# Selective scan: C's rows split into bfloat16 parts in 128x64 tiles, and laid into the spreading table by transfers

## The chip, the cores and the metric

The kernel runs on one core of a Trainium2 chip. The metric is the device time of one execution in microseconds (us); a change is judged by the median of several executions. PE is the matrix engine (PEld its weight loads), DVE the vector engine, ACT the scalar engine, POOL the GpSimd engine, SP the engine that here only issues transfers. SPq and ACTq are the instruction queues of SP and ACT when they issue a DMA.

## The reference, cut to what matters

Four transformer-like layers with an attention-like and an expert block each, on x of shape (8, 512, 128). The change lies in the attention-like block of the third layer, a Mamba block (`L2_attn`), for a batch of 8 sequences of length 512 with 256 inner channels and 16 states:

```python
xdbl = jnp.einsum('bld,de->ble', xc, W_xproj)
dt_r = xdbl[..., :DT_RANK]
Bm = xdbl[..., DT_RANK:DT_RANK + D_STATE]
Cm = xdbl[..., DT_RANK + D_STATE:]
dt = jax.nn.softplus(jnp.einsum('blr,rd->bld', dt_r, W_dt) + b_dt)
A = -jnp.exp(A_log)

def step(h, inp):
    dt_t, B_t, C_t, u_t = inp
    dA = jnp.exp(dt_t[:, :, None] * A)
    h = h * dA + dt_t[:, :, None] * B_t[:, None, :] * u_t[:, :, None]
    y = jnp.einsum('bdn,bn->bd', h, C_t)
    return (h, y)
```

What is computed stays the same: C's values are needed on all 128 partitions, and a float32 value is carried through a bfloat16 matmul as the sum of three bfloat16 parts.

## The kernel before, in words

`build` runs seven layers one after the other, with a barrier between them. `selective_scan` (L2637) is the fifth. Channels lie on partitions in two halves (CH = 2), the sequence of 512 positions along the free axis. The work is a row of M = 128 steps m = 16 q + n: sequence q (0 to 7), state n (0 to 15). A step consists of

- a transfer issued by SP (L2716) that brings B's row n of sequence q from DRAM to all partitions, into one of NB = 4 buffers `bs`;
- on POOL, `dBu` = du * B (L2784), 128x1024, at most ND = 3 steps ahead of the recurrence;
- on ACT, `decay` (L2921), dA = exp(dt * A) in two halves, at most NA = 2 steps ahead;
- on DVE, `recur` (L3020), the scan h over the positions, and for 13 of 16 states `weigh` (L3029), hc = h * C. C's row comes from a bank of PSUM that PE fills by `spread` (L3124), one matmul of the 0/1 table `pick` with `bc`, the spreading table of bfloat16 parts. For the other three states (n = 0, 3, 6) POOL does the multiplication (L2731), with C's row brought by a transfer of SP (L2721) into `c_rows`;
- on PE, `add_up` (L3141), which sums hc into the bank of y.

Between these steps each engine does its part of the preparation of later sequences, at fixed values of n. B and C of sequence q+1 come so: PE's `project` (L3108) makes dt_r, B and C; ACT's `take_bc` (L2871, L2874) copies them from PSUM at n = 0 (at n = 2 for sequence 1) and issues the transfer that stores B and C in DRAM (`b_rows`, L2877). Then the split: `split_first` on ACT (L2882) rounds the 32x512 tile to bfloat16 straight into `bc`, `split_left` on POOL (L2736) takes the remainder, `split_mid` (L2886, ACT) rounds it, `split_last` (L2740, POOL) takes the second remainder, and `split_done` (L2890, L2891, ACT) writes the second and third part into `bc`.

Each engine works its instructions in the order in which they are written, and so does each queue: SP issues one transfer after the other, and where it waits for a semaphore, all transfers written behind wait too. SP waits for `dBu_ready` before it fills a `bs` buffer again (L2715), for the store of B and C at n = 0 (L2713), and for `hp_ready` before it fills `c_rows` again (L2720).

## Time and profile before

| | us |
|---|---|
| median of 3 runs | 2778.79 |
| lowest and highest run | 2772.78 and 2779.42 |
| the profiled execution, its own time | 2771.78 |
| its span in the profile | 2770.0 |
| selective scan, first scan of DVE to last | 900.4 to 1327.0 |
| DVE busy in 1003 to 1057 (one sequence) | 51.77 of 54 |

Times in the profile count from the start of the span. A row of a view names engine, line of the source, operation, output and inputs, and shapes; "xN" is the number of instructions merged in it. Idle time in brackets is what the engine stood still before the row, and behind "<-" stands what ended it.

### The profile page before, as it was taken

What the parts mean: (1) busy time and instruction counts of PE and PEld (TensorE: products, weight loads), DVE (VectorE), ACT (ScalarE), POOL (GpSimd) and SP (SyncE); (2) the same over time, 40 slices, a digit from 0 to 9 for tenths busy, and PEclk for the clock granted to TensorE, in tenths of its full rate; (3) what the DMA queues carried; (4) which work ended last, traced back from release to release, by engine and by line L of the source; (5) the groups of instructions that cost most, each with busy time, mean ns of one, the idle gap of its engine ahead of it and who ended that gap; (6) DMA issues with size and microseconds to landing.
All of it is one profiled execution on the core that took longest, in us unless ns stands there. A gap on an engine that the chain in (4) does not pass through costs nothing. (4 is left out here: it accounts for less than half of the span.)

```text
span 2770.0 us, 42642 instructions
## 1 busy us (share of the span) xinstructions
PE 2480.3 (90%) x13253; PEld 1589.3 (57%) x13280; DVE 1740.7 (63%) x4100; ACT 1433.8 (52%) x2908; POOL 1615.9 (58%) x1421
## 2 busy tenths in 40 slices
PE   7977787799578899997579899999999999999999
PEld 4756777687565344433379734444444445777776
DVE  4436444575424999999756599999999992211112
ACT  3431333334246877775334377777777774333333
POOL 4742555442364999999145376777767771997000
PEclk9988999899788999999889999999999999999999
DMA  9011333500012232322520068888888884000001
GB/s 295 25 35 49 109 107 108 165 1 24 26 40 73 93 98 91 96 97 88 175 80 25 14 142 196 192 191 191 191 195 187 194 193 100 9 16 9 8 8 31
DMA packets 148262, 274.82 MB, mean 99 GB/s; under 512 B 29003, under 2 KB 68694, under 8 KB 148038
## 3 DMA queue, kind: packets, MB, share of 16 engines
q1 hardware_dynamic: 135798, 251.75, 35.2%
q0 software_dynamic: 9088, 18.63, 2.4%
q8 instruction: 109, 1.79, 0.3%
q10 hardware_dynamic: 3152, 1.71, 0.3%
q14 instruction: 115, 0.94, 0.1%
HBM read 102.97 MB, written 24.58 MB: 46 GB/s over the span
## 5 line engine op out<-in xcount | busy, mean ns | idle before, releaser
L1784 POOL TENSOR_TENSOR l3a_p_all<-l3a_p_all,l3a_rden 128x1024 f32<-128x1024 f32 x256 | 483.7, 1893 | 202.2 <-DVE l3a_rden L1859 202.1
L1917 ACT ACTIVATE l3a_p_all<-l3a_p_all,l3a_low 128x512 f32<-128x512 f32 x512 | 364.3, 713 | 129.8 <-DVE l3a_low L1854 128.5
L1854 DVE CUSTOM_DVE_ANT_0 l3a_p_all<-bank,relative_bias 128x512 f32<-128x512 f32 x512 | 331.9, 686 | 53.9 <-PE bank L1983 30.5
L1867 DVE STREAM_TRANSPOSE l3a_blocks<-l3a_p_all 128x1024 f32<-128x1024 f32 x256 | 313.9, 1235 | 1.8 <-issue 1.8
L2784 POOL TENSOR_TENSOR l2a_dBu<-l2a_du,l2a_bs 128x1024 f32<-128x1024 f32 x128 | 298.5, 2352 | 17.4 <-DVE l2a_h L3020 16.2
L3020 DVE TENSOR_TENSOR_SCAN l2a_h<-bank,l2a_dBu 128x1024 f32<-128x1024 f32 x128 | 290.9, 2281 | 11.9 <-POOL l2a_dBu L2784 6.5
L1841 DVE SCALAR_TENSOR_TENSOR x<-bank,l3a_blocks,x 128x128 f32<-128x128 f32 x256 | 71.9, 344 | 336.5 <-PE bank L2058 336.3
L1932 ACT ACTIVATE relative_bias<-bank,l3a_b 128x512 f32<-128x512 f32 x224 | 153.3, 687 | 214.1 <-PE bank L2048 210.8
L1983 PE MATMUL bank<-l3a_kT,l3a_qT 64*128 64x512 f32 x1024 | 245.3, 607 | 3.1 <-DVE l3a_low L1854 2.6
L2009 PE MATMUL bank<-l3a_pT,l3a_v 128*64 128x512 f32 x1024 | 233.8, 598 | 0.1
L2048 PE MATMUL bank<-relative_xnT_all,relative_w_qk 128*128 128x512 f32 x512 | 231.0, 595 | 0.0
L2058 PEld LDWEIGHTS bank<-relative_w_qk,relative_bias 128*128 128x128 f32 x1792 | 208.1, 192 | 25.1 <-issue 25.1
L2058 PE MATMUL bank<-relative_w_qk,relative_bias 128*128 128x128 f32 x1792 | 208.5, 275 | 1.0 <-DVE x L1841 1.0
L3141 PE MATMUL bank<-l2a_hc,ident 128*128 128x512 f32 x416 | 202.9, 612 | 2.5 <-DVE l2a_hc L3029 1.9
L2921 ACT ACTIVATE bank<-l2a_dt,scan_a_neg 128x511 f32<-128x511 f32 x256 | 165.3, 681 | 70.6 <-DVE l2a_h L3020 67.1
L1983 PEld LDWEIGHTS bank<-l3a_kT,l3a_qT 64*128 64x128 f32 x1024 | 98.3, 187 | 148.9 <-issue 139.0
L2048 PEld LDWEIGHTS bank<-relative_xnT_all,relative_w_qk 128*128 128x128 f32 x512 | 93.2, 192 | 93.9 <-issue 93.9
L2009 PEld LDWEIGHTS bank<-l3a_pT,l3a_v 128*64 128x64 f32 x1024 | 67.8, 136 | 120.1 <-issue 111.9
L1207 POOL DMA_INDIRECT l0f_y_rows<-l0fe_y,l0f_target x71 | 75.7, 1066 | 95.5 <-DVE l0fe_y L1276 71.3
L1989 PE MATMUL bank<-relative_xnT_all,relative_w_qk 128*128 128x512 f32 x256 | 128.7, 626 | 2.9 <-issue 2.9
L3141 PEld LDWEIGHTS bank<-l2a_hc,ident 128*128 128x128 f32 x416 | 78.8, 193 | 87.7 <-issue 82.1
L3029 DVE TENSOR_TENSOR l2a_hc<-l2a_h,bank 128x1024 f32<-128x1024 f32 x104 | 124.7, 1199 | 3.7 <-PE bank L3124 3.0
(532 smaller groups left out, 4964.3 us busy)
## 6 DMA issues: line engine op xcount, KB each, us to landing
l3a_pT<-l3a_blocks SPq DMA_DIRECT2D x1024, 128.0 KB
l2a_bs<-l2a_b_rows SPq DMA_DIRECT2D x128, 256.0 KB, 3.1
l0fe_wv<-expert_weights SPq DMA_DIRECT2D x71, 256.0 KB
by_place<-by_distance SPq DMA_DIRECT2D x16, 512.0 KB, 12.6
relative_bias<-by_place SPq DMA_DIRECT2D x16, 448.0 KB, 11.3
...
```

The lines of the kernel that those rows point to most:

```text
L1784: p_ready.by(pool.tensor_tensor(a, a, bcast(rden[g % 2][:, t, :], n_after=S), ALU.mult))
L1854: bk.drain(dve.tensor_tensor_reduce(p_of(g, t)[:, h, :], ps(job)[:], bias[:, u * 2 + h, b0:b0 + S], 1.0, 3.0e38, ALU.add, ALU.min, low[:, ...
L1867: ins = dve.transpose(out, p_of(g, t).rearrange("p h (k b j) -> p (h k) b j", b=Q, j=32))
L1917: ins = act.activation(a, a, ACT.Exp, bias=low[:, t, h:h + 1], scale=-1.0, accum_out=den[:, t, h:h + 1])
L1983: bk.fill(pe.matmul(ps(job)[:], qT[half[h], t * P:(t + 1) * P], kT[half[h], :], start=True, stop=True), job)
L2009: ins = pe.matmul(ps(job)[half[h], :], v[g // GP % 2][:, kt, c:c + DK3], pT[g % 2][:, :, h * TPS + kt, :], start=(kt == 0), stop=(kt == TP ...
L2048: bk.fill(pe.matmul(ps(job)[:], w1[e % 2][:, j * P:(j + 1) * P], xnT_all[:, q * S:(q + 1) * S], start=True, stop=True), job)
L2058: ins = pe.matmul(ps(job)[:, t * D:(t + 1) * D], h[q][:, j, t * P:(t + 1) * P], w2[e % 2][:, j, :], start=(j == 0), stop=(j == J - 1))
L2784: pool.tensor_tensor(dBu[m % ND][:], du[q % 2][:], bcast(bs[m % NB][:], n_before=CH), ALU.mult).then_inc(dBu_ready, 1)
L2921: ins = act.activation(dA[m % NA][:, j, 1:], dt[q % 2][:, j, 1:], ACT.Exp, scale=a_neg[:, j, n:n + 1])
L3020: dve.tensor_tensor_scan(h[m % NH][:].rearrange("p c s -> p (c s)"), dA[m % NA].rearrange("p c s -> p (c s)"), dBu[m % ND][:].rearrange("p ...
L3141: ins = pe.matmul(y_bank[j][:], chip.ident[:], weighed[:, j, :], start=False, stop=(m % N == N - 1))
```

## The change

The tile `raw` (C and B, 32x512) is still copied out of PSUM and stored in DRAM. The split is no longer made on it. SP fetches C's 16 rows back from DRAM as a tile `c_flat` of 128 partitions x 64 elements (each row in 8 pieces); the two remainders on POOL and three roundings on ACT work on 128x64 tiles; and ACT then issues three transfers that lay the three parts into `bc`, 16 rows of 8 pieces of 64 bfloat16 values each. B's rows are no longer split (their rows of `bc` keep the zeros). The steps of the split are moved to later n. The core of the difference:

```diff
@@ -2659,7 +2659,9 @@
         turned = [sb(f"turned{u}", [P, TAPS - 1 + S]) for u in range(3)]
         xc, sz, work = two("xc", [P, CH, S]), sb("sz", [P, CH, S]), sb("work", [P, CH, S])
         dt, du = two("dt", [P, CH, S]), two("du", [P, CH, S])
-        raw, dtr, left, mid = sb("raw", [2 * N, S]), sb("dtr", [R, S]), sb("left", [2 * N, S]), sb("mid", [2 * N, S], BF16)
+        raw, dtr = sb("raw", [2 * N, S]), sb("dtr", [R, S])
+        CUT = N * S // P
+        c_flat, c_left, c_parts = sb("c_flat", [P, CUT]), sb("c_left", [P, CUT]), sb("c_parts", [P, 3, CUT], BF16)
         bc = two("bc", [P, S], BF16)
         bs = [sb(f"bs{k}", [P, S]) for k in range(NB)]
         dBu, h, hc = ([sb(f"{n}{k}", [P, CH, S]) for k in range(c)] for n, c in (("dBu", ND), ("h", NH), ("hc", NC)))
@@ -2706,11 +2709,18 @@
         with nc.Block(no_gpsimd_drain=True) as block:
             @block.sync
             def _(sp):
+                def load_flat(q):
+                    sp.wait_ge(b_stored, 16 * (q + 1))
+                    if q:
+                        sp.wait_ge(left_ready, q)
+                    sp.dma_start(c_flat[:], b_rows[q, N:2 * N, :].rearrange("n (c s) -> (n c) s", s=CUT)).then_inc(flat_loaded, 16)
+
                 answers.load(sp, (0,))
+                load_flat(0)
                 for m in range(M):
                     q, n = divmod(m, N)
-                    if n == 0:
-                        sp.wait_ge(b_stored, 16 * (q + 1))
+                    if n == 5 and q + 1 < B:
+                        load_flat(q + 1)
                     if m >= NB:
                         sp.wait_ge(dBu_ready, m - NB + 1)
                     sp.dma_start(bs[m % NB][:], b_rows[q, n, :].partition_broadcast(P)).then_inc(b_loaded[m % NB], 16)
@@ -2731,13 +2741,15 @@
                     pool.tensor_tensor(hp[k % 2][:], h[m % NH][:], bcast(c_rows[k % 2][:], n_before=CH), ALU.mult).then_inc(hp_ready, 1)
 
                 def split_left(q):
+                    pool.wait_ge(flat_loaded, 16 * (q + 1))
                     pool.wait_ge(hi_ready, q + 1)
-                    pool.wait_ge(raw_ready, q + 1)
-                    pool.tensor_tensor(left[:], raw[:], bc[q % 2][0:2 * N, :], ALU.subtract).then_inc(left_ready, 1)
+                    if q:
+                        pool.wait_ge(low_ready, q)
+                    pool.tensor_tensor(c_left[:], c_flat[:], c_parts[:, 0, :], ALU.subtract).then_inc(left_ready, 1)
 
                 def split_last(q):
                     pool.wait_ge(mid_ready, q + 1)
-                    pool.tensor_tensor(left[:], left[:], mid[:], ALU.subtract).then_inc(left2_ready, 1)
+                    pool.tensor_tensor(c_left[:], c_left[:], c_parts[:, 1, :], ALU.subtract).then_inc(left2_ready, 1)
 
                 def add_step(q, part):
@@ -2785,9 +2797,9 @@
                     if m == 2:
                         late_gains()
                     if q + 1 < B:
-                        if n == (5 if q else 7):
+                        if n == (9 if q else 10):
                             split_left(q + 1)
-                        if n == 10:
+                        if n == (12 if q else 13):
                             split_last(q + 1)
                         if n == 12:
                             add_step(q + 1, slice(0, CH))
@@ -2866,29 +2878,37 @@
                 def take_bc(q):
                     job = ("bc", q)
                     bk.wait_filled(act, job, 0)
-                    if q:
-                        act.wait_ge(left2_ready, q)
                     act.copy(dtr[:], ps(job)[2 * N:2 * N + R, :]).then_inc(dtr_ready, 1)
                     if q:
                         act.wait_ge(b_stored, 16 * q)
                     bk.drain(act.copy(raw[:], ps(job)[0:2 * N, :]), job)
                     bk.wait_read(act, job, 0)
                     act.sem_inc(raw_ready, 1)
+                    act.wait_ge(raw_ready, q + 1)
                     act.dma_start(b_rows[q], raw[:]).then_inc(b_stored, 16)
 
                 def split_first(q):
+                    act.wait_ge(flat_loaded, 16 * (q + 1))
+                    if q:
+                        act.wait_ge(bc_loaded, 48 * q)
+                    act.copy(c_parts[:, 0, :], c_flat[:]).then_inc(hi_ready, 1)
+
+                def split_mid(q):
+                    act.wait_ge(left_ready, q + 1)
+                    act.copy(c_parts[:, 1, :], c_left[:]).then_inc(mid_ready, 1)
+
+                def split_done(q):
+                    act.wait_ge(left2_ready, q + 1)
+                    act.copy(c_parts[:, 2, :], c_left[:]).then_inc(low_ready, 1)
+                    act.wait_ge(cleared, 1)
                     if q >= 2:
                         act.wait_ge(C_ready, (q - 1) * len(of_dve) // B)
-                    act.copy(bc[q % 2][0:2 * N, :], raw[:]).then_inc(hi_ready, 1)
-
-                def split_mid(q):
-                    act.wait_ge(left_ready, q + 1)
-                    act.copy(mid[:], left[:]).then_inc(mid_ready, 1)
-
-                def split_done(q):
-                    act.wait_ge(left2_ready, q + 1)
-                    act.copy(bc[q % 2][PART:PART + 2 * N, :], mid[:])
-                    act.copy(bc[q % 2][2 * PART:2 * PART + 2 * N, :], left[:]).then_inc(bc_ready, 1)
+                    act.wait_ge(hi_ready, q + 1)
+                    act.wait_ge(mid_ready, q + 1)
+                    act.wait_ge(low_ready, q + 1)
+                    for k in range(3):
+                        rows_of_part = bc[q % 2][k * PART + N:k * PART + 2 * N, :]
+                        act.dma_start(rows_of_part.rearrange("n (c s) -> n c s", s=CUT), c_parts[:, k, :]).then_inc(bc_loaded, 16)
 
                 def take_dt(q, j):
                     job = ("dt", q, j)
@@ -2933,16 +2953,15 @@
                 affine(1)
                 turn_to(ACT.Exp)
                 take_bc(0)
-                act.wait_ge(cleared, 1)
-                split_first(0)
                 for j in range(CH):
                     take_dt(0, j)
                 exp_dt(0)
                 log_dt(0)
-                split_mid(0)
+                split_first(0)
                 deviations(2)
                 turn_to(ACT.Exp)
                 act.wait_ge(held.a_ready, 2)
+                split_mid(0)
                 for m in range(NA):
                     decay(m)
                 split_done(0)
@@ -2959,17 +2978,17 @@
                     if q + 1 < B:
                         if n == 0 + late:
                             take_bc(q + 1)
-                        if n == 1 + late:
-                            split_first(q + 1)
                         if n in (3 + late, 4 + late):
                             take_dt(q + 1, n - 3 - late)
                         if n == 5 + late:
                             exp_dt(q + 1)
-                        if n == 6 + late:
+                        if n == 6 + late // 2:
+                            split_first(q + 1)
+                        if n == 9 + late // 2:
                             split_mid(q + 1)
                         if n == 7 + late:
                             log_dt(q + 1)
-                        if n == 11 + late:
+                        if n == 12 + late // 2:
                             split_done(q + 1)
                     if q + 2 < B:
                         if n == 2 + late:
@@ -3118,7 +3137,7 @@
                     if m not in dve_no:
                         return
                     q, n = divmod(m, N)
-                    pe.wait_ge(bc_ready, q + 1)
+                    pe.wait_ge(bc_loaded, 48 * (q + 1))
                     if dve_no[m]:
                         pe.wait_ge(hc_ready, dve_no[m])
                     pe.matmul(c_bank[:], pick[:, n, :], bc[q % 2][:], start=True, stop=True).then_inc(C_ready, 1)
```

Beside this, `bc_ready` is replaced by `bc_loaded` (incremented by 16 by each of the three transfers), and `flat_loaded` and `low_ready` are new semaphores.

Three places of the instruction order on which the prediction rests. SP's queue from the start of the scan, before (L2716 brings B's rows, L2721 C's rows for POOL):

```order
L2716 DMA l2a_bs<-l2a_b_rows 128x512
L2721 DMA l2a_c_rows<-l2a_b_rows 128x512
L2716 DMA l2a_bs<-l2a_b_rows 128x512 x3
L2721 DMA l2a_c_rows<-l2a_b_rows 128x512
L2716 DMA l2a_bs<-l2a_b_rows 128x512 x3
L2721 DMA l2a_c_rows<-l2a_b_rows 128x512
L2716 DMA l2a_bs<-l2a_b_rows 128x512 x10
```

and of the change (L2716 is now the load of `c_flat`, L2726 brings B's rows, L2731 C's):

```order
L2716 DMA l2a_c_flat<-l2a_b_rows 128x64
L2726 DMA l2a_bs<-l2a_b_rows 128x512
L2731 DMA l2a_c_rows<-l2a_b_rows 128x512
L2726 DMA l2a_bs<-l2a_b_rows 128x512 x3
L2731 DMA l2a_c_rows<-l2a_b_rows 128x512
L2726 DMA l2a_bs<-l2a_b_rows 128x512
L2716 DMA l2a_c_flat<-l2a_b_rows 128x64
L2726 DMA l2a_bs<-l2a_b_rows 128x512 x2
L2731 DMA l2a_c_rows<-l2a_b_rows 128x512
```

The second load of `c_flat` (sequence 1) now stands ahead of the B rows of steps 5 and 6, and so it does in each later sequence for the next. POOL's queue in sequence 0 from step 5 on, before (L2731 is the multiplication with C's rows):

```order
L2784 TENSOR_TENSOR l2a_dBu<-l2a_du,l2a_bs 128x1024 x3
L2736 TENSOR_TENSOR l2a_left<-l2a_raw,l2a_bc 32x512
L2731 TENSOR_TENSOR l2a_hp<-l2a_h,l2a_c_rows 128x1024
L2784 TENSOR_TENSOR l2a_dBu<-l2a_du,l2a_bs 128x1024 x3
L2740 TENSOR_TENSOR l2a_left<-l2a_left,l2a_mid 32x512
L2731 TENSOR_TENSOR l2a_hp<-l2a_h,l2a_c_rows 128x1024
L2784 TENSOR_TENSOR l2a_dBu<-l2a_du,l2a_bs 128x1024 x2
```

and of the change (L2741 is that multiplication, L2796 is dBu):

```order
L2796 TENSOR_TENSOR l2a_dBu<-l2a_du,l2a_bs 128x1024 x3
L2741 TENSOR_TENSOR l2a_hp<-l2a_h,l2a_c_rows 128x1024
L2796 TENSOR_TENSOR l2a_dBu<-l2a_du,l2a_bs 128x1024 x3
L2748 TENSOR_TENSOR l2a_c_left<-l2a_c_flat,l2a_c_parts 128x64
L2741 TENSOR_TENSOR l2a_hp<-l2a_h,l2a_c_rows 128x1024
L2796 TENSOR_TENSOR l2a_dBu<-l2a_du,l2a_bs 128x1024 x2
```

Both remainders are narrower and stand one group of dBu later. ACT near the end of a sequence, before (L2827 copies a convolution, L2842 copies z):

```order
L2890 COPY l2a_bc<-l2a_mid 32x512
L2891 CAST l2a_bc<-l2a_left 32x512
L2827 ACTIVATE l2a_xc<-bank,scan_packed 128x512
L2921 ACTIVATE bank<-l2a_dt,scan_a_neg 128x511 x2
L2842 COPY l2a_sz<-bank 128x512
L2921 ACTIVATE bank<-l2a_dt,scan_a_neg 128x511 x2
L2842 COPY l2a_sz<-bank 128x512
```

and of the change (L2941 is decay, L2839 the convolution, L2854 z):

```order
L2839 ACTIVATE l2a_xc<-bank,scan_packed 128x512
L2941 ACTIVATE bank<-l2a_dt,scan_a_neg 128x511 x2
L2902 CAST l2a_c_parts<-l2a_c_left 128x64
L2911 DMA l2a_bc<-l2a_c_parts 16x8x64 x3
L2854 COPY l2a_sz<-bank 128x512
L2941 ACTIVATE bank<-l2a_dt,scan_a_neg 128x511 x2
L2854 COPY l2a_sz<-bank 128x512
```

The end of the split moved behind the second convolution and the next decay, right ahead of the first copy of z.

## Rows read from the trace of the kernel before

**Rows 1.** Stretches: columns PE, PEld, DVE, ACT, POOL busy, PEclk, DMA share, GB/s.

```profile
910.00:914.00 4.00, 4.00 (x7) 1.34 (x6) 3.92 (x3) 3.14 (x6) 4.00 (x3) 0.60 0.03 10
1003.00:1057.00 54.00, 50.88 (x131) 22.43 (x134) 51.77 (x33) 41.46 (x63) 51.12 (x24) 0.97 0.30 95
```

**Rows 2.** Groups of DVE in 897 to 1332: busy, mean ns | idle before, releaser.

```profile
L3020 DVE TENSOR_TENSOR_SCAN l2a_h<-bank,l2a_dBu 128x1024 f32<-128x1024 f32 x128 | 290.9, 2281 | 11.9 <-POOL l2a_dBu L2784 6.5 <-ACT bank L2921 5.3
L3029 DVE TENSOR_TENSOR l2a_hc<-l2a_h,bank 128x1024 f32<-128x1024 f32 x104 | 124.7, 1199 | 3.7 <-PE bank L3124 3.0 <-remote 0.4
```

**Rows 3.** Waits in 900 to 1330: us in total, times, longest us.

```profile
POOL l2a_dBu L2784 <- DVE l2a_h L3020: 16.2, 15, 1.6
```

**Rows 4.** SP in order of time, 886 to 926: start, us.

```profile
889.31 0.34 SPq L2716 DMA_DIRECT2D l2a_bs<-l2a_b_rows  x1
...
900.31 4.94 SPq L2716 DMA_DIRECT2D l2a_bs<-l2a_b_rows  x3
912.81 0.32 SPq L2721 DMA_DIRECT2D l2a_c_rows<-l2a_b_rows  x1
913.18 12.63 SPq L2716 DMA_DIRECT2D l2a_bs<-l2a_b_rows  x6
```

**Rows 5.** ACT in order of time, sequences 0 and 1.

```profile
887.64 0.33 ACTq L2877 DMA_DIRECT2D l2a_b_rows<-l2a_raw  x1
888.01 0.62 ACT L2882 CAST l2a_bc<-l2a_raw 32x512 bf16<-32x512 f32 x1 [0.48 <-ACT l2a_raw L2874]
...
896.26 0.32 ACT L2804 ACTIVATE l2a_std<-l2a_mv,ln_eps 128x24 f32<-128x24 f32 x1
...
898.20 2.51 ACT L2921 ACTIVATE bank<-l2a_dt,scan_a_neg 128x511 f32<-128x511 f32 x4
...
913.21 0.32 ACTq L2877 DMA_DIRECT2D l2a_b_rows<-l2a_raw  x1
```

**Rows 6.** POOL in order of time, sequence 0.

```profile
904.86 0.28 POOL L2765 TENSOR_TENSOR l2a_shifts<-l2a_inv,l2a_mv 128x48 f32<-128x48 f32 x1
...
912.75 6.96 POOL L2784 TENSOR_TENSOR l2a_dBu<-l2a_du,l2a_bs 128x1024 f32<-128x1024 f32 x3
...
931.33 1.15 POOL L2740 TENSOR_TENSOR l2a_left<-l2a_left,l2a_mid 32x512 f32<-32x512 f32 x1 [1.25 <-ACT l2a_mid L2886]
```

**Rows 7.** Landing of B's rows: all 128 loads, then those at 913.4:913.9.

```profile
DMA to landing us min/median/max: 3.0/3.1/5.7
DMA to landing us min/median/max: 4.0/4.0/4.0
```

**Rows 8.** DVE in order of time, sequence 0.

```profile
915.18 2.29 DVE L3020 TENSOR_TENSOR_SCAN l2a_h<-bank,l2a_dBu 128x1024 f32<-128x1024 f32 x1 [1.26 <-POOL l2a_dBu L2784]
...
948.77 2.29 DVE L3020 TENSOR_TENSOR_SCAN l2a_h<-bank,l2a_dBu 128x1024 f32<-128x1024 f32 x1 [1.23 <-POOL l2a_dBu L2784]
```

**Rows 9.** PE in order of time, sequence 0.

```profile
919.51 0.38 PE L3124 MATMUL bank<-l2a_bc,scan_pick 128*128 128x512 bf16 x1 [0.35 <-DVE l2a_hc L3029]
...
929.10 0.38 PE L3124 MATMUL bank<-l2a_bc,scan_pick 128*128 128x512 bf16 x1 [2.02 <-DVE l2a_hc L3029]
```

**Rows 10.** Start of sequence 3: ACT's store, POOL's dBu of step 5, DVE.

```profile
1069.42 0.31 ACTq L2877 DMA_DIRECT2D l2a_b_rows<-l2a_raw  x1
1073.98 2.35 POOL L2784 TENSOR_TENSOR l2a_dBu<-l2a_du,l2a_bs 128x1024 f32<-128x1024 f32 x1
1076.93 4.46 DVE L3020 TENSOR_TENSOR_SCAN l2a_h<-bank,l2a_dBu 128x1024 f32<-128x1024 f32 x2
```

**Rows 11.** ACT at the end of sequence 3.

```profile
1106.12 1.29 ACT L2921 ACTIVATE bank<-l2a_dt,scan_a_neg 128x511 f32<-128x511 f32 x2
1108.33 0.59 ACT L2842 COPY l2a_sz<-bank 128x512 f32<-128x512 f32 x1 [0.92 <-PE bank L3101]
...
1111.12 0.58 ACT L2842 COPY l2a_sz<-bank 128x512 f32<-128x512 f32 x1 [0.61 <-PE bank L3101]
1111.72 1.28 ACT L2847 ACT_TABLE_LOAD   x1
```

5 lines of the change are left out of this document (3 added, 2 removed).

## Prediction

> **What bounds the kernel now.** I read the scan stage alone, since nothing else is touched. First the stretches: while sequence 2 is worked, DVE is busy 51.8 of 54 us at a granted clock of 0.97, POOL 51.1, PE 50.9, ACT only 41.5 [rows 1]. So DVE sets the pace, POOL and PE are close behind it, ACT has room. Then the groups of DVE: over 128 steps its scans of 2.28 us and its multiplications of 1.20 us make 416 us, and it waits just 11.9 us in front of scans: 6.5 for POOL's dBu and 5.3 for ACT's decay [rows 2]. Then the waits the other way: POOL stands still 16.2 us in 15 places because it is already three steps ahead of DVE [rows 3]. Work taken off ACT and POOL in the steady state is therefore worth next to nothing. What counts is whether the change makes DVE wait somewhere.
>
> **What it removes.** For each sequence ACT loses four 32x512 operations of 0.60 to 0.62 us (L2882 is one) [rows 5] and gets three of 128x64. The nearest small one, 128x24, takes 0.32 us [rows 5], so about 1.5 us less. POOL loses two subtractions of 1.15 us and gets two of 128x64; the nearest, 128x48, takes 0.28 [rows 6]: 1.7 us less. In sequences 1 to 7 the cover is that POOL waits for DVE anyway [rows 3]: I cost the relief at 0. Only in sequence 0 does POOL hold DVE back (waits of 1.26 and 1.23 us for dBu [rows 8]); there it counts, below.
>
> **What it adds on SP.** SP now issues the load of `c_flat` for sequence q+1 ahead of B's row of step n = 5, and that load waits until ACT has stored B and C. SP runs ahead of everybody: the rows of steps 4 to 6 went out from 900.31 on, as soon as a buffer was free [rows 4]. ACT's store for sequence 1 is issued only at 913.21 [rows 5]. So the queue stands still behind it, and with it B's rows of steps 5 to 8, until the store is through. From the first store to what waited for it, 887.64 to 889.31 [rows 5, 4], a store takes 1.67 us: 913.21 + 1.67 = 914.88. The issue of `c_flat` takes 0.34 us and a gap [rows 4], say 0.4: B's row of step 5 is issued at 915.3. Loads land after 3.0 to 5.7 us, median 3.1; one with others just ahead of it took 4.0 [rows 7]. Here four more transfers of 256 KB and a small one crowd the same moment, so I take 4.0: landed at 919.3. POOL began dBu of step 5 at 912.75 [rows 6]. It starts 6.55 us late; with 3.0 or 5.7 us it would be 5.55 or 8.25.
>
> **What of it reaches the end of sequence 0.** POOL is fully booked from step 5 to step 14 but for one wait of 1.25 us, for ACT's rounding ahead of L2740 [rows 6]. With the new places (rounding at n = 7 and 10, subtractions at n = 10 and 13) that wait should be gone. POOL wins it back, and 2 x (1.15 - 0.28) = 1.74 us of narrower subtractions: 3.0 together. dBu of step 14 is then 6.55 - 3.0 = 3.6 us late (bounds 2.6 and 5.3), and DVE's scan 14 waited for exactly that dBu (948.77, 1.23 us [rows 8]), so it moves to 952.4. DVE alone could be there a little earlier: scan 5 at 915.18 + 6.55 = 921.7, then nine scans and eight multiplications, 9 x 2.28 + 8 x 1.20 = 30.1 us, make 951.8. From then on DVE is the bound and has nothing to make the loss up with: **+3.6 us**.
>
> **Later sequences.** The same queue order returns. For sequence 3 the store goes out at 1069.42 and POOL's dBu of step 5 starts at 1073.98; DVE's scan 5, the second of the merged pair, at 1079.1 [rows 10]. By the same sum, B's row lands at 1069.42 + 1.67 + 0.4 + 4.0 = 1075.5, POOL starts 1.5 us late and delivers 2.35 us later, at 1077.9: 1.2 us before DVE wants it. Right behind it POOL no longer has the subtraction at n = 5. So 0; with a landing of 5.7 us DVE would wait 0.5 us in each of some six sequences, 3 us in all.
>
> **The start.** ACT's rounding at 888.01 leaves the way to the first step sizes (0.62 us [rows 5]), and a second one leaves ahead of the first decays; in return POOL's first dBu now stands behind a subtraction that waits for a rounding placed after ACT's table change. These cancel within half a microsecond: 0, bounds -0.5 and +0.5. C's parts come by transfers: after the two first decays (2.51 us from 898.20 [rows 5]), a cast and three issues they leave by about 902 and land by 905.1 at 3.1 us; DVE wants the first C after three scans from 900.4, at 907.2. Covered.
>
> **ACT at the end of a sequence.** Decay ends at 1107.4 [rows 11]; a cast of 0.3 and three issues at ACT's 0.31 to 0.33 us [rows 5, 10] end at about 1108.8, where the copy of z stood at 1108.33. Copy, decay and second copy (0.59 + 1.30 + 0.58) then end at 1111.3; the table load came at 1111.72 [rows 11]. Covered, with 0.4 us to spare: 0.
>
> **Sum.** 3.6 us on the profiled execution: 2771.8 + 3.6 = 2775.4. That execution lies at the low edge of the runs, whose median is 2778.79; on it the sum is 2782.4. That is 0.13%. What a measurement of this kernel can tell from no change is about 0.3%, 8.3 us.
>
> The rows give a store 1.67 us and a crowded load 4.0. The Trainium skill, "DMA: Bandwidth & Descriptors", section "Anatomy of one DMA — SWDGE (gpsimd) path", gives 2.0 us fixed plus bytes/436e3, for the GpSimd path. By it the store would take 2.15 and the load 2.6 us, dBu 5 would be 5.65 us late, and the sum 2.7 instead of 3.6. No row here shows a load of 256 KB below 3.0, so the rows decide.
>
> **Rivals.**
> - *The late load is hidden and POOL's relief shows.* If the queue does not stand still, or lands in time, sequence 0 keeps what POOL saves, at most 3.0 us; DVE's last wait for dBu there was 1.23 [rows 8]. Time: 2775.8 to 2777.6. Against it: 10 us and more lie between the buffers that came free by about 904.9 (900.31 + 4.94 less an issue [rows 4]) and the store. Chance 0.10.
> - *PE becomes the bound after the stall.* PE's `spread` of step 5 stood at 919.51 and waits for DVE's multiplication behind scan 5; now at 925.2. PE idles 5.7 us and has only 2.02 us of waiting later to make up for it [rows 9], and after an idle stretch the granted clock was 0.60 of 2.4 GHz in 910 to 914 [rows 1], so mostly at the 1.2 GHz level, which costs 4 x 0.4 = 1.6 us of work. PE would then be 5.3 us late and DVE with it: 2784.1. Chance 0.13.
> - *ACT's three issues are the new wait (slower).* They stand ahead of the z copies that the last table loads of each sequence wait for. The issues must end by 1111.72 - 2.47 = 1109.25; from 1107.8 (with a little for the semaphore) that allows 0.48 us each. SP shows 0.34 and ACT 0.31 for plain rows [rows 4, 10]; 128 pieces of 128 bytes have no row. Beyond 0.48 each tenth costs 0.3 us in six or seven sequences. At 0.95 us it is 1.4 x 6 = 8.4 us: 2790.8. Chance 0.12, with half of it above the 0.3% line.
> - *Every step-5 load lands at 5.7 us.* 5.3 + 3 = 8.3 us: 2787.1. Chance 0.05.
>
> On the third rival, the Trainium skill's same page, section "Issuing engines are not separate DMA queues", says the issuing time is usually small beside the transfer. By it the rival would be worth nothing; no run here shows it for this pattern yet.
>
> **How the numbers follow.** My case has 0.60; its own range is +2.6 to +5.3. Faster than 0.3% would need 8.3 us, more than the 6.5 us that DVE waits for POOL: I leave 0.03 of the first rival's 0.10 for it. Slower than 0.3%: half of the third rival, half of the fourth, and 0.04 for both mild ones together with a sum above mine: 0.13. Within: the rest, 0.84. The range: down to 2773, a run at the low edge with the relief nearly full; up to 2790, near the third rival's time.
>
> **What would show it.** In the new profile: SP's second load of `c_flat` at about 914.9 and B's row of step 5 at 915.3; POOL's dBu of step 5 at about 919 with a wait for a DMA; DVE's scan 5 at 921 to 922 with an idle of 6 to 8 us; scan 14 near 952.4; sequence 1 onwards at the old spacing of 54 us; DVE's total wait in front of scans up by about 3.6. Wrong if ACT's end of a sequence grows, if PE's waits vanish and DVE waits for `spread`, or if the spacing of later sequences changes.

## The result, and the profile after

| | before | after |
|---|---|---|
| median of 22 runs each, us | 2778.49 | 2784.85 |
| lowest and highest run | 2772.78, 2786.84 | 2775.41, 2794.99 |
| ratio after / before, 95% interval | | 1.0022 (1.0014 to 1.0030) |
| the profiled execution, its own time | 2771.78 | 2794.99 |
| its span | 2770.0 | 2793.2 |
| first scan of DVE to the last one's start | 424.35 | 432.05 |

The change costs about 6 us: 2784.85 where 2782.4 was forecast, within 0.3% of before. The profiled execution of after is the slowest of its 22 runs, so its span can't be set against that of before: of the 23.2 us between the two, 11.6 lie ahead of the first scan and 3.9 behind the last, in stages that neither version changes. Only the scan stage is compared here, from the start of DVE's first scan to the start of its last: **7.7 us longer**.

The groups of DVE in the scan stage of after (columns as in the rows ahead of the prediction; against [rows 2]):

```profile
L3039 DVE TENSOR_TENSOR_SCAN l2a_h<-bank,l2a_dBu 128x1024 f32<-128x1024 f32 x128 | 290.7, 2279 | 19.0 <-POOL l2a_dBu L2796 11.3 <-ACT bank L2941 7.6
L3048 DVE TENSOR_TENSOR l2a_hc<-l2a_h,bank 128x1024 f32<-128x1024 f32 x104 | 124.5, 1197 | 6.1 <-PE bank L3143 5.7
...
L3060 DVE TENSOR_TENSOR x<-bank,x 128x512 f32<-128x512 f32 x7 | 4.8, 683 | 3.6 <-PE bank L3169 3.6
```

DVE's own work is unchanged, 290.7 and 124.5 us. It waits more, for three engines: for POOL's dBu 11.3 us (6.5 before), for ACT's decay 7.6 (5.3), for PE's row of C 5.7 (3.0). The first pair holds the wait ahead of the first scan, 3.54 us (2.23 before), which lies outside the stage: inside it the waits for POOL are 7.8 us (4.3 before). To see where, cut the stage into sequences, from DVE's scan 0 of one to scan 0 of the next, and sum the idle brackets in each:

| sequence | 0 | 1 | 2 | 3 | 4 | 5 | 6 |
|---|---|---|---|---|---|---|---|
| length before | 55.02 | 54.16 | 54.05 | 54.05 | 54.04 | 52.87 | 51.73 |
| length after | 60.42 | 56.66 | 53.21 | 53.45 | 54.37 | 54.39 | 51.46 |
| DVE waits for ACT, before | 0.24 | 1.85 | 0.75 | 0.76 | 0.75 | 0.76 | 0.23 |
| DVE waits for ACT, after | 0 | 3.00 | 1.10 | 1.34 | 1.08 | 1.10 | 0 |
| DVE waits for y's sum on PE, before | 0 | 0 | 1.19 | 1.20 | 1.18 | 0 | 0 |
| DVE waits for y's sum on PE, after | 0 | 1.19 | 0 | 0 | 1.20 | 1.20 | 0 |

So two losses: 5.4 us in sequence 0, and 2.3 us in the rest of the stage, where DVE's waits for ACT rise from 5.1 to 7.6 us; together the 7.7. Of the 5.4 in sequence 0, DVE waits 3.5 us more for POOL and 2.6 more for PE's rows of C, and 0.6 less in small waits. The waits in the last two rows come and go between sequences, but sum to the same 3.6 us; the section on the hardware returns to them.

**Sequence 0.** SP's queue in after, 908 to 932 us, against [rows 4]:

```profile
911.88 0.32 SPq L2726 DMA_DIRECT2D l2a_bs<-l2a_b_rows  x1
926.11 0.32 SPq L2716 DMA_DIRECT2D l2a_c_flat<-l2a_b_rows  x1
926.47 0.91 SPq L2726 DMA_DIRECT2D l2a_bs<-l2a_b_rows  x2
927.42 0.43 SPq L2731 DMA_DIRECT2D l2a_c_rows<-l2a_b_rows  x1
927.90 0.91 SPq L2726 DMA_DIRECT2D l2a_bs<-l2a_b_rows  x2
```

Nothing leaves between 911.88 and 926.11. ACT's store went out at 924.47, `c_flat` follows 1.64 us later, and B's rows of steps 5 and on come out in a burst behind it. POOL and DVE after the stall:

```profile
929.78 6.96 POOL L2796 TENSOR_TENSOR l2a_dBu<-l2a_du,l2a_bs 128x1024 f32<-128x1024 f32 x3 [5.40 <-DMA l2a_bs<-l2a_b_rows]
...
945.93 0.30 POOL L2748 TENSOR_TENSOR l2a_c_left<-l2a_c_flat,l2a_c_parts 128x64 f32<-128x64 f32 x1
949.11 2.37 POOL L2741 TENSOR_TENSOR l2a_hp<-l2a_h,l2a_c_rows 128x1024 f32<-128x1024 f32 x1 [2.89 <-PE bank L3160]
```

```profile
932.20 2.29 DVE L3039 TENSOR_TENSOR_SCAN l2a_h<-bank,l2a_dBu 128x1024 f32<-128x1024 f32 x1 [6.71 <-POOL l2a_dBu L2796]
...
946.78 1.22 DVE L3048 TENSOR_TENSOR l2a_hc<-l2a_h,bank 128x1024 f32<-128x1024 f32 x1 [3.06 <-PE bank L3143]
...
965.75 2.29 DVE L3039 TENSOR_TENSOR_SCAN l2a_h<-bank,l2a_dBu 128x1024 f32<-128x1024 f32 x1 [0.74 <-POOL l2a_dBu L2796]
```

POOL waits 5.40 us for B's row, DVE 6.71 for dBu. That is the stall as forecast. What follows it is the rival that was given a chance of 0.13: at 946.78 DVE waits 3.06 us for PE, and POOL 2.89 at 949.11. PE in the same time, and its stretches (columns as in [rows 1]):

```profile
935.75 0.58 PE L3143 MATMUL bank<-l2a_bc,scan_pick 128*128 128x512 bf16 x1 [6.68 <-DVE l2a_hc L3048]
936.13 3.62 PE L3160 MATMUL bank<-l2a_hc,ident 128*128 128x512 f32 x4
...
941.68 3.78 PE L3160 MATMUL bank<-l2a_hc,ident 128*128 128x512 f32 x4
...
948.99 1.88 PE L3160 MATMUL bank<-l2a_hc,ident 128*128 128x512 f32 x4
```

```profile
928.00:936.00 8.00, 1.32 (x4) 0.53 (x4) 3.80 (x3) 2.40 (x6) 6.22 (x3) 0.66 0.63 200
936.00:944.00 8.00, 8.00 (x10) 2.71 (x10) 7.41 (x4) 4.52 (x8) 8.00 (x5) 0.50 0.30 83
944.00:952.00 8.00, 8.00 (x20) 3.79 (x18) 5.22 (x4) 6.63 (x13) 5.11 (x4) 0.78 0.24 68
```

PE stood idle 6.68 us behind the stall and came back at a granted clock of 0.50, the 1.2 GHz level: four matmuls of `add_up` take 3.62 to 3.78 us there, 1.88 once the clock is back. PE is busy 8.00 of 8.00 us and is the bound for that time.

**Sequences 1 to 6.** SP's queue stands behind the store in each of them too. POOL's waits for a row of B in the whole stage:

```profile
POOL l2a_dBu L2796 <- DMA l2a_bs<-l2a_b_rows: 12.7, 7, 5.4
```

Beside the 5.40 us of sequence 0 these are 2.19 in sequence 1 and 0.83 to 1.35 in each of the sequences 2 to 6; before has none. DVE does not feel them: it has no wait for dBu behind sequence 0. What it feels is ACT. ACT at the end of sequence 3 in after, against [rows 11]; then the transfers of the parts in the view of the tile `c_parts` (duration in ns: least, median, most; first and last start):

```profile
1123.57 1.29 ACT L2941 ACTIVATE bank<-l2a_dt,scan_a_neg 128x511 f32<-128x511 f32 x2
1124.79 0.23 ACT L2902 CAST l2a_c_parts<-l2a_c_left 128x64 bf16<-128x64 f32 x1
1125.13 2.12 ACTq L2911 DMA_DIRECT2D l2a_bc<-l2a_c_parts  x3
1127.35 0.58 ACT L2854 COPY l2a_sz<-bank 128x512 f32<-128x512 f32 x1 [2.33 <-issue]
...
1129.76 1.28 ACT L2859 ACT_TABLE_LOAD   x1
```

```profile
L2911 ACTq DMA_DIRECT2D l2a_bc<-l2a_c_parts x24: 554/618/830, 911.9 to 1287.7; - x24
```

The three issues hold ACT for 2.12 us. From the decay's start the table load comes 1129.76 - 1123.57 = 6.19 us later, where before it was 1111.72 - 1106.12 = 5.60 [rows 11]. The next decays come behind it, and DVE waits for them; of the same wait, before and then after:

```profile
1063.61 2.29 DVE L3020 TENSOR_TENSOR_SCAN l2a_h<-bank,l2a_dBu 128x1024 f32<-128x1024 f32 x1 [0.75 <-ACT bank L2921]
```

```profile
1082.25 2.29 DVE L3039 TENSOR_TENSOR_SCAN l2a_h<-bank,l2a_dBu 128x1024 f32<-128x1024 f32 x1 [1.10 <-ACT bank L2941]
```

### The profile page after: what moved, and what is told of

The parts are those of the page before. It is cut to its first block and busy times, and to the rows that moved or that the text cites. A ratio compares the mean times of both kernels' runs of the same rounds, so it can differ in the third digit from the quotient of the medians.

```text
span 2793.2 us, 42683 instructions
## 1 busy us (share of the span) xinstructions
PE 2496.4 (89%) x13253; PEld 1598.4 (57%) x13280; DVE 1740.9 (62%) x4100; ACT 1419.0 (51%) x2900; POOL 1603.1 (57%) x1421
## 3 DMA queue, kind: packets, MB, share of 16 engines
q10 hardware_dynamic: 6608, 2.11, 0.4%
## 5 line engine op out<-in xcount | busy, mean ns | idle before, releaser
L2796 POOL TENSOR_TENSOR l2a_dBu<-l2a_du,l2a_bs 128x1024 f32<-128x1024 f32 x128 | 298.9, 2356 | 32.0 <-DVE l2a_h L3039 19.3
L3039 DVE TENSOR_TENSOR_SCAN l2a_h<-bank,l2a_dBu 128x1024 f32<-128x1024 f32 x128 | 290.7, 2279 | 19.0 <-POOL l2a_dBu L2796 11.3
L2941 ACT ACTIVATE bank<-l2a_dt,scan_a_neg 128x511 f32<-128x511 f32 x256 | 165.2, 682 | 76.5 <-DVE l2a_h L3039 72.8
L3048 DVE TENSOR_TENSOR l2a_hc<-l2a_h,bank 128x1024 f32<-128x1024 f32 x104 | 124.5, 1197 | 6.1 <-PE bank L3143 5.7
```

The source lines that it names most:

```text
L2796: pool.tensor_tensor(dBu[m % ND][:], du[q % 2][:], bcast(bs[m % NB][:], n_before=CH), ALU.mult).then_inc(dBu_ready, 1)
L2941: ins = act.activation(dA[m % NA][:, j, 1:], dt[q % 2][:, j, 1:], ACT.Exp, scale=a_neg[:, j, n:n + 1])
L3039: dve.tensor_tensor_scan(h[m % NH][:].rearrange("p c s -> p (c s)"), dA[m % NA].rearrange("p c s -> p (c s)"), dBu[m % ND][:].rearrange("p ...
```

## The experiments

The theory: SP's queue, standing behind the store, costs sequence 0 some 5 to 6 us; narrower work on POOL gives a part back; and the three issues on ACT cost each later sequence a third to half a microsecond. The rivals: PE's fall to 1.2 GHz carries the loss rather than the queue, and the rest is only noise between executions. The kernels were timed on three chips, each beside runs of before on the same chip. The levels of the chips differ (before had medians of 2691.44, 2695.64 and 2780.34 us there), so times are compared by ratio on one chip and traces by the length of the scan stage, which is 424.35 us in the profile of before. A range behind a ratio is its 95% interval.

One thing for reading the expectations: where they speak of DVE's waits for ACT of 2.2 to 2.4 us and of 1.5, the wait at each border between two sequences is counted in both of them. In the counting of the table above these are 1.1 to 1.2 and 0.75.

### flat_late: the load of c_flat behind B's later rows

```diff
-                    if n == 5 and q + 1 < B:
+                    if n == (7 if q else 8) and q + 1 < B:
                         load_flat(q + 1)
```

> The changed kernel, but SP issues the load of c_flat at n = 8 (sequence 0) and n = 7 (others) instead of n = 5, where the store of B and C should have landed already. Theory (the queue stands still behind the store, and PE's slow clock after it eats what POOL saves): POOL's wait of 5.4 us for B's row of step 5 is gone, PE stays at the 2.4 GHz level there, sequence 0 takes 52.5 to 55 us instead of 60.4, sequence 1 about 55 instead of 56.7, and from first to last scan 425 to 428.5 us instead of 432.05 (before: 424.35). DVE's waits for ACT at the end of each sequence stay at 2.2 to 2.4 us. Rival (the loss comes from the places of the split or the narrower tiles, not from the queue): sequence 0 stays near 60 us.

Ratio 1.0012 (1.0000 to 1.0024). Scan stage 425.76; sequence 0 takes 52.13 us, 8.3 less than after and 2.9 less than before. POOL at the place of the stall, and DVE's scans:

```profile
843.25 2.36 POOL L2741 TENSOR_TENSOR l2a_hp<-l2a_h,l2a_c_rows 128x1024 f32<-128x1024 f32 x1
845.57 6.99 POOL L2796 TENSOR_TENSOR l2a_dBu<-l2a_du,l2a_bs 128x1024 f32<-128x1024 f32 x3
```

```profile
L3039 DVE TENSOR_TENSOR_SCAN l2a_h<-bank,l2a_dBu 128x1024 f32<-128x1024 f32 x128 | 290.7, 2279 | 13.8 <-ACT bank L2941 7.4 <-POOL l2a_dBu L2796 6.3
```

dBu of step 5 follows without a wait, and the longest idle time of PE in sequence 0 is 1.70 us. So the whole of sequence 0's loss hangs on the place of that one load, and the relief of POOL is real: 2.9 us, near the upper end of what the first rival was priced at. The wait for ACT stays at 7.4: it has another cause. The stage is still 1.4 us longer than before: -2.9 in sequence 0, +2.1 for ACT, +2.2 more of waits for y's sum (6.0 against 3.8). Sequence 1 takes 56.28 us, not the 55 that were expected: it has a wait of 1.19 us for y's sum, and 2.81 us of waits for ACT.

### before_wait: the wait alone, in the kernel before

```diff
                         sp.wait_ge(b_stored, 16 * (q + 1))
+                    if m == 5:
+                        sp.wait_ge(b_stored, 32)
                     if m >= NB:
```

> The kernel before with one line more: SP waits for the store of sequence 1's B and C ahead of B's row of step 5, and nothing else. Theory: the wait alone makes the stall: POOL 5 to 5.5 us late at step 5, DVE about 6.5 us idle, then PE at the 1.2 GHz level for some 10 us; sequence 0 takes 60 to 62 us instead of 55.0, the later ones as before, first to last scan 429.5 to 432 us, the run 5.5 to 7.5 us slower than before. Rival A (the loss is won back as the prediction had it): sequence 0 at 57.5 to 58.7. Rival B (the loss belongs to other parts of the change): no difference.

Ratio 1.0038 (1.0026 to 1.0050). Scan stage 429.77; sequence 0 takes 60.12 us, 5.1 more than before, the others differ from before by at most 1.2 us, the size of one wait for y's sum. The wait alone makes the stall (POOL waits 5.11 us for B's row), with no transfer, cast or issue of the change in the kernel. Here nothing is won back. POOL still has its wide subtractions, and a wait for ACT between them, as the repeat of this kernel shows further down. PE comes back slow here too (a granted clock of 0.81 from 853 to 861), but DVE does not wait for it in sequence 0: POOL is the bound. The ratio is larger than 5.4 us of a scan stage explain (0.0020); the repeat below did not show it again.

### six_issues: three further issues on ACT

From sequence 1 on, ACT issues the same three transfers once more, into a table that nobody reads; the counts of the semaphore follow.

```diff
+                    if q:
+                        for k in range(3):
+                            act.dma_start(spare[k * PART + N:k * PART + 2 * N, :].rearrange("n (c s) -> n c s", s=CUT), c_parts[:, k, :]).then_inc(bc_loaded, 16)
```

> The changed kernel, but ACT issues the three parts a second time into an unused table, for sequences 1 to 7 (six issues of 0.69 us instead of three). Theory (ACT's issuing time is on the path at the end of a sequence): each sequence 1 to 6 gets 1.8 to 2.1 us longer and DVE's waits for ACT there rise from 2.2 to 2.4 us to above 4 us; in all 11 to 14 us slower than the changed kernel. Rival (the issues are covered by ACT's waits, the larger waits of the changed kernel are something else): below 3 us in all.

Ratio 1.0080 (1.0061 to 1.0099). Scan stage 443.62, 11.6 more than after. ACT at the end of a sequence, and DVE's groups:

```profile
1040.33 1.88 ACTq L2912 DMA_DIRECT2D l2a_bc<-l2a_c_parts  x3
1042.24 1.92 ACTq L2915 DMA_DIRECT2D l2a_spare<-l2a_c_parts  x3
1044.26 0.58 ACT L2855 COPY l2a_sz<-bank 128x512 f32<-128x512 f32 x1 [4.03 <-issue]
```

```profile
L3043 DVE TENSOR_TENSOR_SCAN l2a_h<-bank,l2a_dBu 128x1024 f32<-128x1024 f32 x128 | 290.7, 2279 | 18.1 <-POOL l2a_dBu L2797 11.7 <-ACT bank L2945 6.3
L3052 DVE TENSOR_TENSOR l2a_hc<-l2a_h,bank 128x1024 f32<-128x1024 f32 x104 | 124.9, 1201 | 19.0 <-PE bank L3147 18.5
```

A second set costs the same on ACT, 1.92 us. It is paid in another place: DVE waits not for ACT (6.3) but for PE (18.5, against 5.7), since ACT's copy of z is late, PE waits for the bank that it drains (2.02 us at 1044.90), and the spread behind it in PE's order is late too. Behind that wait PE is slow as well: granted clock 0.61 from 1045 to 1049, and 3.36 us for four matmuls of `add_up`. The stage is longer by what was expected (11 to 14 us), but not by the wait that was expected (ACT's above 4 us per sequence), and the sequences 1 to 6 grow by 0.9 to 3.8 us over after, not evenly. So doubling doesn't double the loss; it moves to an engine with even less room. The place of these issues is a sensitive one, but this run is no ruler for the price of the first three.

### one_issue: one transfer of parts instead of three

```diff
-                    for k in range(3):
+                    for k in range(1 if q else 3):
```

> The changed kernel, but for sequences 1 to 7 ACT issues only the transfer of the first part (C is then used in plain bfloat16 there: the two smaller parts are left out). Theory: ACT is 1.4 us earlier at the end of each sequence, DVE's waits for ACT return from 2.2 to 2.4 us to about 1.5 us, sequences 1 to 6 get 0.6 to 0.9 us shorter, 4 to 5.5 us in all; sequence 0 stays at about 60 us. Rival (DVE's wait there is set by PE or the table loads): no change beyond 1 us.

Ratio 1.0030 (1.0013 to 1.0046). Scan stage 429.82.

```profile
L3039 DVE TENSOR_TENSOR_SCAN l2a_h<-bank,l2a_dBu 128x1024 f32<-128x1024 f32 x128 | 290.6, 2279 | 17.3 <-POOL l2a_dBu L2796 11.5 <-ACT bank L2941 5.7
```

The waits for ACT fall to 0.76 us in each of the sequences 2 to 5, the value of before, and the total to 5.7. With the flat_late run this separates the two losses: the place of the load moves only sequence 0, the number of issues only the waits for ACT. The stage is 2.2 us shorter than in after, 1.2 of it in sequence 0; 4 to 5.5 us were expected. In sequence 1 the waits for ACT stay at 2.69 us (3.00 in after, 1.86 before). The 0.31 us that go are those of the scan at its end; the rest of the rise lies at its step 1, where DVE waits 1.46 us in after, in one_issue and in six_issues alike, and 0.63 before. That part does not go with the number of issues. The ratio can't show it; it is larger than after's, with a wide interval.

### keep_pe and dt_early: is it PE's clock?

`keep_pe` lets PE work through the stall on matmuls of no use. To have a point at which they may start, a pair of ACT's operations is taken ahead of the decays; `dt_early` does that move alone.

```diff
                     late = 0 if q else 2
+                    if m == 5:
+                        take_dt(1, 0)
                     decay(m + NA)
...
-                        if n in (3 + late, 4 + late):
+                        if n in (3 + late, 4 + late) and m != 5:
                             take_dt(q + 1, n - 3 - late)
```

and in `keep_pe` alone:

```diff
                         keep_running(1, chip.psum[7])
+                    if m == 4:
+                        bk.wait_read(pe, ("dt", 1, 0), 0)
+                        keep_running(6, chip.psum[7])
                     spread(m + 1)
```

> The changed kernel with only ACT's copy of that step-size bank ahead of the decay, and no dummy products: the control of the run with them. Theory: PE idles and falls to the 1.2 GHz level as in the changed kernel; sequence 0 at 59 to 60.5 us. Rival (the copy's new place is what helps): 58 us or less.

> The changed kernel with the same stall, but PE does not stand still in it: ACT copies the first step-size bank of sequence 1 ahead of a decay, and PE then runs six dummy products of 0.85 us into that bank until the stall ends. Theory (the slow clock of PE after its 6.7 us of idling eats what POOL saves): PE stays at the 2.4 GHz level after the stall, DVE's wait of 3.06 us for C and POOL's of 2.89 us for PE vanish, sequence 0 takes 57.5 to 58.5 us instead of 60.4, first to last scan 429 to 430.5 instead of 432.05. Rival (DVE and POOL cannot win anything back after the stall whatever PE does): sequence 0 stays at 59.5 to 60.5.

dt_early ran once and has no ratio: 2709.5 us, scan stage 432.87, sequence 0 59.03. keep_pe: ratio 1.0014 (1.0002 to 1.0025), scan stage 428.77, sequence 0 57.79. PE in keep_pe, and its stretches:

```profile
850.93 7.11 PE L3177 MATMUL bank<-scan_packed,ident 128*128 128x512 f32 x12 [1.36 <-ACT l2a_dt L2919]
857.88 0.38 PE L3145 MATMUL bank<-l2a_bc,scan_pick 128*128 128x512 bf16 x1
858.09 1.88 PE L3162 MATMUL bank<-l2a_hc,ident 128*128 128x512 f32 x4
```

```profile
849.00:857.00 8.00, 6.64 (x12) 2.58 (x11) 4.07 (x3) 2.99 (x6) 6.51 (x3) 0.79 0.61 197
857.00:865.00 8.00, 8.00 (x23) 3.34 (x21) 7.66 (x5) 5.24 (x9) 8.00 (x5) 1.00 0.24 80
```

PE waits 1.36 us ahead of the dummy products and the clock falls for some 3 us (0.79 in the first stretch), but it is back before the stall ends. Where the real work begins again, at 857.88, the granted clock is 1.00 and `add_up` takes 1.88 us for four at once. DVE's waits for PE in sequence 0 are gone (3.29 us in after, 2.14 in dt_early, none in keep_pe). What stays is 57.79 - 55.02 = 2.8 us: the stall's own cost after POOL has won back what it can. So PE's clock is a real part of the loss in the profiled execution of after (60.42 - 57.79 = 2.6 us), but not its cause: without it the stall still costs.

One execution of each would not show this, since after_again, further down, has 57.78 us with no dummy products. But six profiled executions have the same stall and the same POOL work behind it, and the length of sequence 0 follows DVE's wait for PE's rows of C. The clock is that of the 8 us from 4 us behind the start of DVE's scan 5:

| | keep_pe | after_again | dt_early | one_issue | six_issues | after |
|---|---|---|---|---|---|---|
| granted clock | 1.00 | 0.77 | 0.50 | 0.50 | 0.50 | 0.50 |
| DVE waits for C in sequence 0, us | 0 | 0.45 | 2.14 | 2.11 | 2.40 | 3.29 |
| length of sequence 0, us | 57.79 | 57.78 | 59.03 | 59.21 | 59.39 | 60.42 |

In after the slow level also lasts longest: over the next 8 us its clock is 0.79, that of the others 0.96 to 1.00.

### flat_late_sp: the load late, and the parts issued by SP

```diff
-                    if n == 5 and q + 1 < B:
+                    if n == (7 if q else 8) and q + 1 < B:
                         load_flat(q + 1)
+                    if n == 2 and q:
+                        lay_parts(sp, q)
...
+                    if q == 0:
+                        lay_parts(act, q)
```

Here `lay_parts` holds the waits and the three `dma_start` that ACT had.

> The changed kernel with the load of c_flat at n = 8 or 7, and the three parts of sequences 1 to 7 issued by SP at n = 2 of their own sequence instead of by ACT at the end of the one before. Theory (two mechanisms, the queue and ACT's issuing time, make the whole loss): DVE's waits for ACT at the end of a sequence return to about 1.5 us, the sequences 1 to 6 to 54.1 us and less, sequence 0 stays near 52.1; first to last scan 420 to 423.5 us, 1 to 4 us below the kernel before, so at best just measurable. Rival (SP's three issues of 0.7 us delay B's rows of step 2 and on): POOL waits for bs in each sequence, 2 us each.

Ratio 1.0006 (0.9996 to 1.0015). Scan stage 421.45, 2.9 us less than before. Three views: DVE's group of scans, ACT at the end of a sequence, and the transfers in the view of the table `bc` with the time from issue to landing:

```profile
L3045 DVE TENSOR_TENSOR_SCAN l2a_h<-bank,l2a_dBu 128x1024 f32<-128x1024 f32 x128 | 290.6, 2279 | 12.1 <-POOL l2a_dBu L2809 6.7 <-ACT bank L2947 5.4
```

```profile
1030.56 1.29 ACT L2947 ACTIVATE bank<-l2a_dt,scan_a_neg 128x511 f32<-128x511 f32 x2
...
1036.17 1.28 ACT L2872 ACT_TABLE_LOAD   x1
```

```profile
L2718 SPq DMA_DIRECT2D l2a_bc<-l2a_c_parts x21: 552/598/662, 873.7 to 1193.5; - x21
DMA to landing us min/median/max: 1.8/1.9/3.0
```

The table load is back at 5.61 us behind the decay, and the waits for ACT at 5.4 us, both as before (0.76 us in each of the sequences 2 to 5; sequence 1 keeps 2.32, against 1.86 before). SP needs 0.60 us for such an issue, as ACT needs 0.62, but nobody waits behind it there (POOL waits for a row of B once, 0.2 us): the time goes with the transfer and not with the engine, and only its place in the order makes it a cost. Which trait of the transfer it is, its small pieces or that it stays within SBUF, no run separates.

### flat_late_mid: the load late, and the split earlier

```diff
-                    if n == 5 and q + 1 < B:
+                    if n == (7 if q else 8) and q + 1 < B:
                         load_flat(q + 1)
...
-                        if n == (9 if q else 10):
+                        if n == (8 if q else 10):
                             split_left(q + 1)
-                        if n == (12 if q else 13):
+                        if n == (10 if q else 13):
                             split_last(q + 1)
...
-                        if n == 6 + late // 2:
+                        if n == (4 if q else 7):
                             split_first(q + 1)
-                        if n == 9 + late // 2:
+                        if n == (6 if q else 10):
                             split_mid(q + 1)
...
-                        if n == 12 + late // 2:
+                        if n == (10 if q else 13):
                             split_done(q + 1)
```

> The changed kernel with the load of c_flat at n = 8 or 7, and in sequences 1 to 6 the whole split some steps earlier, so that ACT issues the three parts after the decay of n = 10, where it waits about 2 us for DVE anyway. Theory (what matters is where ACT's 2 us of issuing stand): the same as with SP issuing: DVE's waits for ACT at 1.5 us, sequences 2 to 6 at 54.1 us or less, first to last scan 421 to 424.5 us. Rival (ACT's time is short everywhere in the second half of a sequence): the waits stay at 2.2 us or more.

Ratio 1.0002 (0.9989 to 1.0016). Scan stage 422.70.

```profile
L3039 DVE TENSOR_TENSOR_SCAN l2a_h<-bank,l2a_dBu 128x1024 f32<-128x1024 f32 x128 | 290.7, 2279 | 11.9 <-POOL l2a_dBu L2796 6.3 <-ACT bank L2941 5.5
```

ACT issues the same 24 transfers at the same price (median 0.62 us), but from sequence 1 on two steps earlier and not right ahead of the copies of z. DVE's waits for ACT are 0.76 us again in each of the sequences 2 to 5. That settles for them what the one_issue run left open: it is not the issues that cost but the issues at that place. Sequence 1 keeps 2.49 us: the wait at its end is 0.76 too, but that at its step 1 is 1.25 (1.08 in flat_late_sp, 0.63 before). What makes that one is not shown.

### The repeats: before_again, after_again, before_wait_again, flat_late_sp_again

The same kernels once more, all four on one chip.

> The kernel before, unchanged, timed against itself, to see what the method makes of no change at all, and whether the scan's length repeats. Expected: ratio 1.000 with 1 inside an interval of about +-0.1%; first to last scan 424.35 us within 1.3 us (the 1.2 us wait of DVE for PE at the output's sum comes in some sequences and not in others).

> The changed kernel, unchanged, on this chip. Expected from its first profile: first to last scan 432.05 us within 1.3 us, sequence 0 at 59 to 60.5 us, about 7.7 us above the kernel before in the scan, so a ratio of 1.0029; the span before the scan, 912 us in its first profile, back to what the kernel before has on this chip, since the change does not touch it.

> The kernel before with SP's one wait, timed again: the first time gave a ratio of 1.0038 where its scan was just 5.4 us longer (1.0020). Expected if the wait costs what the scan shows: a ratio of 1.0015 to 1.0025. If it costs something outside the scan too: 1.003 and more again, and the profile shows it in another stage.

> The changed kernel with the late load of c_flat and SP issuing the parts, timed again. Its scan was 2.9 us shorter than that of the kernel before (0.9989), its runs gave 1.0006 with an interval of 0.9996 to 1.0015. Expected if the scan tells the whole: 0.998 to 1.0005; first to last scan 421.45 us within 1.3.

| run | ratio, 95% interval | scan stage | sequence 0 | ahead of the first scan |
|---|---|---|---|---|
| before_again | 0.9997 (0.9986 to 1.0007) | 425.14 | 55.01 | 903.6 |
| after_again | 1.0022 (1.0012 to 1.0033) | 431.67 | 57.78 | 912.0 |
| before_wait_again | 1.0020 (1.0009 to 1.0032) | 429.58 | 60.80 | 912.5 |
| flat_late_sp_again | 0.9985 (0.9975 to 0.9995) | 420.97 | 52.12 | 905.9 |

The 1.0022 of after came again, the 1.0038 of before_wait did not: 1.0020, near what 4.4 to 5.2 us of scan stage give (0.0016 to 0.0019). Two expectations on after_again failed: sequence 0 took 57.78 us, not 59 to 60.5, and the time ahead of the first scan did not return to that of before. But before_wait_again has the same code as before ahead of the scan and took 8.9 us more there than before_again (912.5 against 903.6). And in the two first profiles the difference is there before the changed layer begins: DVE's first instruction of it stands at 865.28 in before and at 877.69 in after, 12.4 us later. So the 11.6 us are not the change's work in that layer; where they come from is not known. POOL in before_wait_again, after the stall:

```profile
930.64 6.96 POOL L2786 TENSOR_TENSOR l2a_dBu<-l2a_du,l2a_bs 128x1024 f32<-128x1024 f32 x3 [5.77 <-DMA l2a_bs<-l2a_b_rows]
...
949.19 1.15 POOL L2742 TENSOR_TENSOR l2a_left<-l2a_left,l2a_mid 32x512 f32<-32x512 f32 x1 [1.23 <-ACT l2a_mid L2888]
```

It has the wait of 1.23 us for ACT's rounding and the subtractions of 1.15 us that after no longer has. after_again, the same kernel as after, has the same stall (POOL waits 5.62 us) but other stretches behind it:

```profile
928.00:936.00 8.00, 1.19 (x3) 0.29 (x2) 3.51 (x3) 2.15 (x5) 5.94 (x3) 0.83 0.60 191
936.00:944.00 8.00, 7.96 (x17) 3.33 (x18) 7.68 (x5) 5.38 (x10) 8.00 (x5) 0.74 0.29 92
944.00:952.00 8.00, 7.95 (x20) 3.56 (x20) 8.00 (x7) 7.95 (x14) 8.00 (x5) 1.00 0.25 71
```

From 936 to 944 the clock was 0.74, where after had 0.50, and from 944 on 1.00, where after had 0.78. DVE waits 0.45 us for PE in sequence 0 instead of 3.29. Sequence 0 takes 57.78 us, what keep_pe had with PE kept at work.

**A version that beats both.** flat_late_sp was 2777.60 us against 2780.34 of before on this chip, a ratio of 0.9985; on the chip of its first timing it was 1.0006, with 1 inside its interval. Its scan stage is 2.9 to 4.2 us shorter than that of before in all four pairings of their profiles, that is 0.10 to 0.15%. It beats after clearly (0.9985 against 1.0022 on the same chip); that it beats before rests on the scan stage and one of two timings.

## Why the prediction was right, and where it was not

- **What bounds the kernel.** Right. DVE's work is the same, and the loss is the sum of its waits. Outside sequence 0 DVE waited for no dBu, before or after, so POOL's relief there gave nothing.
- **The queue stands still behind the store.** Right, step by step. Store to `c_flat` 1.64 us (forecast 1.67), to B's row 0.36 (0.4), landing 929.78 - 926.47 = 3.3 (4.0). dBu of step 5 is 5.45 us late against the first scan (6.55), DVE's scan waits 6.71 us (6 to 8). before_wait shows that the wait alone does it, flat_late that with the load further behind there is no stall. One number there was off and changed nothing: between the buffers free by 904.9 and the store's issue at 913.21 lie 8.3 us; it is 10 only to the end of the store. On this landing the Trainium skill, "DMA: Bandwidth & Descriptors", section "Anatomy of one DMA — SWDGE (gpsimd) path", would give, as an estimate from a fit made for GpSimd's path while SP and ACT issue here, 2.6 us, and 2.15 for the store; the trace has 3.3 and 1.64, and the measurement decides.
- **What POOL wins back.** Right in size: 3.0 us forecast. flat_late shows 2.9 without the stall, and between before_wait (60.12, 60.80) and after_again or keep_pe (57.78, 57.79) lie 2.3 to 3.0 with it.
- **Sequence 0 in all: +3.6 (bounds 2.6 to 5.3).** Measured +2.8 in after_again and keep_pe, +4.0 in dt_early, +4.2 in one_issue, +4.4 in six_issues, +5.4 in after. The forecast assumed that DVE and PE follow POOL at full speed. They do not always: the second rival, PE as the bound, was written as a case of its own with 5.3 us, and it is what the profile of after shows (5.4). It was wrong to set it beside the forecast as another way: it is the same mechanism with a size that differs from execution to execution, 0 to 2.6 us on top.
- **Later sequences, B's row late.** Right. POOL was to start 1.5 us late; it waits 2.19 us for a row of B in sequence 1 and 0.83 to 1.35 in each of the sequences 2 to 6, and DVE doesn't feel it; its waits for dBu lie in sequence 0 alone.
- **The start.** Right: from ACT's first store to the first scan 12.85 us, 12.75 before, +0.1. Casts took 0.23 us (0.32 taken), narrow subtractions 0.30 (0.28).
- **ACT at the end of a sequence: 0.** This is the term that failed. The issues were taken at 0.31 to 0.33 us, from rows of plain transfers; they took 2.12 us for three, 0.71 each, beyond the limit of 0.48 that the third rival named. That rival's sum, (0.71 - 0.48) x 3 = 0.69 us in the table load, was near: 0.59 measured. But DVE felt only a part, 0.3 to 0.6 us in sequences 2 to 5 and 1.14 in sequence 1, less 0.23 in sequence 6 and 0.24 in sequence 0: 2.3 us in all, not some 4.5. Of this the waits at the ends of the sequences 1 to 5, 1.9 us together, are shown to come from the place of the issues (flat_late_mid, flat_late_sp); the 0.83 us more at step 1 of sequence 1 are not explained by it. By the prediction's own signs this part is wrong: ACT's end of a sequence grew, and DVE's waits in front of scans rose by 7.1 us (11.9 to 19.0), of which 1.3 lie ahead of the first scan, not by 3.6. The bracket between the two prices was open in the prediction, and the row chosen was the nearest in engine, not in form. The Trainium skill, same page, section "Issuing engines are not separate DMA queues", says that the issuing time is usually small beside the transfer. Here it was 0.60 us beside 1.9 to landing, a third, and on ACT it stood in the path; for this pattern the traces do not agree with the rule.
- **The sum.** Sequence 0 +2.8 to +5.4 and ACT +2.3 make 5.1 to 7.7, beside 6 us in the medians. 3.6 was forecast. Against the middle executions (+4.0 to +4.4 in sequence 0) most of what is missing is ACT's term. That the total fell inside the range says little for this term: the range went up to 2790.

Not settled: the ratios of flat_late, one_issue, flat_late_mid and the first flat_late_sp (1.0012, 1.0030, 1.0002, 1.0006) are each 0.0007 to 0.0017 higher than their scan stages would give. Each may be the scatter of the unchanged stages, which differed by up to 12 us between executions; no run was made for it. That the store could be issued earlier on ACT wasn't tried either.
